# A pre-norm decoder layer on one core: loads split and reordered, buffer clearing moved, value projection written straight into two partition halves

## What is computed

```python
n = layernorm(x)
q, k, v = n @ Wq.T, n @ Wk.T, n @ Wv.T            # 16 heads of 16 features
s = q k^T / 4;  s = where(key > query, -inf, s) + alibi(head)
x = x + softmax(s) v @ Wo.T + bo
n = layernorm(x)
x = x + softmax(where(mask, n ctx^T / 16, -1e30)) ctx
n = layernorm(x)
up, down = mxfp4(W_up), mxfp4(W_down)             # block scales and 4-bit codes, blocks of 32 rows
x = x + gelu(n @ up) @ down + b_down
```

## Time and profile before

| | us |
|---|---|
| median of 3 runs | 162.13 |
| lowest and highest run | 159.33 and 162.51 |
| span of the profiled execution, first to last instruction | 157.1 |

### The profile page before, as it was taken

The page is one execution under the profiler, slowest core; times in us unless marked ns, Lnnn a source line. Parts: engine busy times, 40 slices in busy tenths (PEclk is TensorE's granted clock), DMA queues, the critical chain, the costliest instruction groups (busy, mean ns, idle before and its releaser), DMA issues. The chain is left out here.

```text
span 157.1 us, 2931 instructions
## 1 busy us (share of the span) xinstructions
PE 127.9 (81%) x878; PEld 87.3 (56%) x878; DVE 126.1 (80%) x345; ACT 96.4 (61%) x212; POOL 54.1 (34%) x92
## 2 busy tenths in 40 slices
PE   0149999987992497991977999898999999979992
PEld 0027444312471174550565657677788989759991
DVE  1854998799999999779899988796785789697551
ACT  3014559996936045582322742666989899899970
POOL 8969920052211240310403343732540254052000
PEclk9999999999999789998579999999999999999999
DMA  4999993000020341910000000000000000020011
GB/s 95 321 329 341 368 274 144 2 2 4 2 67 0 87 180 30 280 30 0 0 0 4 0 0 0 4 2 0 4 0 2 4 33 31 3 73 0 0 67 67
DMA packets 9135, 11.20 MB, mean 71 GB/s; under 512 B 1665, under 2 KB 7937, under 8 KB 8993
## 3 DMA queue, kind: packets, MB, share of 16 engines
q1 hardware_dynamic: 7776, 9.90, 20.3%
q10 hardware_dynamic: 1344, 1.13, 2.2%
HBM read 9.45 MB, written 1.05 MB: 67 GB/s over the span
## 5 line engine op out<-in xcount | busy, mean ns | idle before, releaser
L556 POOL TENSOR_TENSOR s_sb<-s_sb,s_max 128x512 f32<-128x512 f32 x16 | 17.3, 1084 | 50.1 <-DVE s_max L828 50.1
L969 PE MATMUL bank<-k,q_T 128*64 128x512 f32 x64 | 20.0, 681 | 5.2 <-DVE s_sb L825 5.2
L1064 PE MATMUL bank<-xn_T,w_T 128*128 128x256 f16 x128 | 19.2, 273 | 1.2 <-ACT h_sb L688 0.7
L1080 PE MATMUL bank<-w_down_q,h_hi 128*128 128x256 f32 x64 | 18.7, 318 | 0.0
L636 ACT ACTIVATE p_T<-bank 128x512 f32<-128x512 f32 x16 | 9.6, 599 | 13.1 <-PE bank L990 10.3
L932 PE MATMUL bank<-const,xn 128*128 128x128 f32 x48 | 10.3, 304 | 8.8 <-DVE xn L785 8.7
L990 PEld LDWEIGHTS bank<-v,p_T 128*64 128x64 f32 x256 | 14.1, 148 | 5.9 <-issue 4.7
L902 DVE TENSOR_TENSOR h_lo<-h_sb,h_hi 128x256 fp32r<-128x256 f32 x32 | 13.4, 437 | 4.8 <-ACT h_sb L688 4.8
L528 POOL TENSOR_SCALAR var_eps<-mean_var 128x1 f32<-128x1 f32 x24 | 5.8, 240 | 31.7 <-DVE mean_var L777 31.6
L688 ACT ACTIVATE h_hi<-bank,bias_cols 128x256 fp32r<-128x256 f32 x32 | 15.3, 478 | 2.3 <-PE bank L1080 0.7
L990 PE MATMUL bank<-v,p_T 128*64 128x34 f32 x256 | 15.7, 235 | 1.2 <-ACT q_T L643 1.1
(11 more groups left out here) (82 smaller groups left out, 271.6 us busy)
## 6 DMA issues: line engine op xcount, KB each, us to landing
raw<-in_W_up_T_dram SPq DMA_DIRECT2D x1, 1024.0 KB, 10.5
ctx_T<-in_ctx_by_feature_dram SPq DMA_DIRECT2D x1, 1024.0 KB, 9.7
ctx_sb<-in_ctx_dram SPq DMA_DIRECT2D x1, 1024.0 KB, 9.9
raw<-in_W_up_dram SPq DMA_DIRECT2D x1, 1024.0 KB, 4.9
raw<-in_W_down_T_dram SPq DMA_DIRECT2D x1, 1024.0 KB, 4.8
raw<-in_W_down_dram SPq DMA_DIRECT2D x1, 1024.0 KB, 6.6
out_dram<-x_sb SPq DMA_DIRECT2D x8, 128.0 KB, 1.7
x_sb<-in_x_dram SPq DMA_DIRECT2D x4, 128.0 KB, 3.1
```

The costliest lines, as they stand in the source:

```text
L556: pool.tensor_tensor(tile, tile, s_max[:, u % S_RING, :].unsqueeze(2).broadcast_to([P, HC, S]), ALU.subtract).then_inc(centred, 1)
L969: last = pe.matmul(dst[b * S:(b + 1) * S, :].rearrange("p (h k) -> p h k", h=HC), q_T[:, c, tok], k2[:, c, :, tok], start=True, stop=True)
L1064: last = pe.matmul(dst[:, 0:GN], w_up_q[:, c, f * P:(f + 1) * P], xn_T16[:, g * GT:(g + 1) * GT, at16:at16 + P], start=(k == 0), stop=(k = ...
L1080: last = pe.matmul(dst, src[:, i % H_RING, t * P:(t + 1) * P], w_down_q[:, f, :], start=(f == 0 and part == 0 and t == 0), stop=(f == FC - ...
```

## The change

It has four parts.

Loads: Wv is loaded alone, first behind the constants; then the bias columns, Wq and Wk, and Wo alone. SP waits for Wv before it issues x tiles 4 to 7 and all that follows, and alibi goes ahead of W_up_T. The semaphore for Wv and Wo becomes two.

Clearing: in the planner `x_fill` and the `v2_zero` of the second half come after the last `add_bo`. The instructions are the same.

Values: the rows of Wv are ordered on the host so that all even heads come first, then all odd ones. `v` uses 64 tokens of one sequence as weights and 128 columns of Wv as the moving operand, and writes even heads (j = 0) into partitions 0 to 63 of the bank and odd heads into 64 to 127: 16 calls for a pair of tiles in place of 4. One copy on ACT (`v_even`) and one on DVE (`v_odd`), each of 64 partitions by 512, then fill `v2`. `v_copy`, `v_own`, `v_move`, `v_spread` and the buffers `v_out` and `v_moved` are gone.

Order: some costs in `stages()` and nearly all weights in `URGENCY` are new.

```diff
@@ -85,11 +85,11 @@
             add("low", (t,), "dve", 0.35, [("turn_copy", (n, t))])
 
     for t in range(HALF + 1):
-        add("load_x", (t,), "dma", 2.3 if t == 0 else 0.9 if t < HALF else 2.5)
-
-    queues = {"dma": (("load_x", 0.0), ("load_row_biases", 0.6), ("load_rows", 0.6), ("load_up", 3.5),
-                      ("load_alibi", 1.0), ("load_mask", 1.0), ("load_ctx", 6.0)),
-              "dma2": (("load_biases", 4.0), ("load_qk", 3.0), ("load_vo", 1.5))}
+        add("load_x", (t,), "dma", 2.0 if t == 0 else 0.7 if t < HALF else 2.5)
+
+    queues = {"dma": (("load_x", 0.0), ("load_row_biases", 0.6), ("load_rows", 0.6), ("load_alibi", 1.0),
+                      ("load_up", 3.5), ("load_mask", 1.0), ("load_ctx", 6.0)),
+              "dma2": (("load_v", 4.5), ("load_biases", 0.2), ("load_qk", 1.5), ("load_o", 3.0))}
     for queue, loads in queues.items():
         before = []
         for name, us in loads:
...
@@ -118,13 +118,12 @@
                 add("k_rest", (h, c), "dve", 0.46 * (HC - K_HEADS[h, c]), [("k_flat", (h, c)), ("qk_bias", ())])
             keys[h, c] = copies
         for pair in range(2):
-            add("v", (h, pair), "pe", 1.75, turned[:2 * pair + 2] + [("load_vo", ())], [v_bank(h, pair)], ("v_own", (h, pair)))
-            add("v_copy", (h, pair), "act", 0.55, [("v", (h, pair))] + ([("v_move", (0,))] if h else []))
-            add("v_own", (h, pair), "dve", 0.7, [("v_copy", (h, pair)), ("v2_zero", (h,))])
-        add("v_move", (h,), "sp", 2.5, [("v_copy", (h, 1))] + ([("v_spread", (0,))] if h else []))
-        add("v_spread", (h,), "act", 1.0, [("v_move", (h,)), ("v2_zero", (h,))])
-        add("v2_zero", (h,), "pool", 2.6)
-    add("x_fill", (), "pool", 0.9)
+            add("v", (h, pair), "pe", 1.75, turned[:2 * pair + 2] + [("load_v", ())], [v_bank(h, pair)],
+                [("v_even", (h, pair)), ("v_odd", (h, pair))])
+            add("v_even", (h, pair), "act", 0.55, [("v", (h, pair)), ("v2_zero", (h,))])
+            add("v_odd", (h, pair), "dve", 0.6, [("v", (h, pair)), ("v2_zero", (h,))])
+        add("v2_zero", (h,), "pool", 2.6, [("add_bo", (TILES - 1,))] if h else [])
+    add("x_fill", (), "pool", 0.9, [("add_bo", (TILES - 1,))])
     add("rows_copy", (), "act", 1.1, [("load_rows", ())])
     add("qk_bias", (), "dve", 0.4, [("load_biases", ())])
 
...
@@ -140,13 +139,13 @@
         add("prob_copy", (u,), "act", 0.5, [("prob_T", (u,))] + ([("pv", (u - 2,))] if u >= 2 else []))
 
         reused = [("attn_turn", (u - 2,))] if u >= 2 else []
-        add("pv", (u,), "pe", 0.6, [("prob_copy", (u,)), ("v_spread", (h,)), ("v_own", (h, 1))] + reused, [4],
+        add("pv", (u,), "pe", 0.6, [("prob_copy", (u,)), ("v_even", (h, 1)), ("v_odd", (h, 1))] + reused, [4],
             ("normalise", (u,)))
         add("normalise", (u,), "dve", 0.45, [("pv", (u,))])
         add("attn_turn", (u,), "pe", 0.08, [("normalise", (u,))], [ATTN_BANK], ("attn_copy", (u,)))
         add("attn_copy", (u,), "act", 0.27, [("attn_turn", (u,))])
     for t in range(TILES):
-        add("out_proj", (t,), "pe", 0.9, [("attn_copy", (EC * t + EC - 1,))], [5], ("x1", (t,)))
+        add("out_proj", (t,), "pe", 0.9, [("attn_copy", (EC * t + EC - 1,)), ("load_o", ())], [5], ("x1", (t,)))
         add("x1", (t,), "dve", 0.4, [("out_proj", (t,)), ("add_bo", (t,))])
         layer_norm(LN2, t, [("x1", (t,))])
         add("x_scores", (t,), "pe", 0.45, [("turn_copy", (LN2, t)), ("load_ctx", ())], [7], ("x_mask", (t,)))
...
@@ -212,12 +211,16 @@
 PE_BUSY = 0.385
 
 URGENCY = {
-    "x_fill": 23, "add_down": 23, "v2_zero": 22, "norm": 18, "q": 17, "turn": 16, "attn_copy": 14,
-    "load_qk": 12, "final": 9, "load_mask": 6, "load_vo": 6, "spread_copy": 5, "pv": 5, "gelu": 5,
-    "out_proj": 3, "turn_copy": 3, "low": 3, "normalise": 2, "k_flat": 1, "prob_copy": 1, "x2": 1,
-    "load_rows": 0, "x_prob_copy": 0, "k_rest": 0, "x_read": -1, "stats": -1, "qk_bias": -1, "k_copy": -1,
-    "x_scale": -2, "q_copy": -2, "rstd": -2, "add_bo": -2, "x_mask": -2, "split": -2, "v_own": -4,
-    "scale_T": -9, "prob_T": -12,
+    "turn_copy": 78, "load_v": 52, "v_even": 48, "x_fill": 38, "x_read": 35, "attn_turn": 33, "normalise": 30,
+    "k_rest": 28, "load_o": 27, "split": 23, "amax": 23, "load_ctx": 22, "norm": 21, "centre": 19, "gelu": 18,
+    "prob_copy": 17, "x_mask": 17, "x1": 16, "x_prob_T": 15, "spread_copy": 13, "store": 13, "reload": 13,
+    "load_qk": 12, "low": 12, "rstd": 10, "add_down": 7, "turn": 7, "final": 6, "load_vo": 6, "load_rows": 3,
+    "spread": 3, "up": 3, "x_scores": 3, "q_copy": 2, "attn_copy": 1, "load_alibi": -1, "v2_zero": -2,
+    "x_exp": -3, "pv": -4, "add_bo": -4, "v_own": -4, "load_row_biases": -7, "load_up": -8, "load_biases": -10,
+    "quant": -13, "out_proj": -15, "load_mask": -16, "scores": -16, "down": -16, "x2": -19, "scale_T": -19,
+    "prob_T": -20, "k_copy": -26, "exp": -26, "k": -26, "load_x": -27, "binade": -29, "v_odd": -32,
+    "x_prob_copy": -39, "k_flat": -41, "qk_bias": -42, "q": -43, "add_max": -43, "scale_copy": -44,
+    "x_table": -59, "v": -100, "x_scale": -165,
 }
 
 
...
@@ -455,6 +451,15 @@
             return xn_T[:, h * HALF:(h + 1) * HALF, c * P:(c + 1) * P]
+
+        def v2_tiles(h, pair):
+
+            first = h * B // 2 + 4 * pair
+            return v2[:, first:first + 4, :, :, :]
+
+        def v_tiles(h, pair):
+
+            return bank[v_bank(h, pair)][:, :].rearrange("p (b g d) -> p b g d", b=4, d=D)
 
         def keys_copied(h, c):
...
@@ -466,14 +471,15 @@
         def _(sp):
             for t in range(HALF):
                 sp.dma_start(x_sb[:, t, :], x_tiles[t]).then_inc(x_loaded[t], 16)
+            sp.wait_ge(v_loaded, 16)
             sp.dma_start(x_sb[:, HALF:TILES, :], x_tiles[HALF:TILES].rearrange("t p e -> p t e")).then_inc(
                 x_loaded[HALF], 16)
             sp.dma_start(row_biases_all[:, :, :], row_biases.unsqueeze(0).broadcast_to([P, 2, E])).then_inc(
                 bias_loaded, 16)
             sp.dma_start(rows_f, block_of_row).then_inc(rows_loaded, 16)
+            sp.dma_start(alibi_sb[:, :, :], alibi).then_inc(alibi_loaded, 16)
             sp.dma_start(raw[:, :].rearrange("p (c k) -> p c k", c=FC),
                          W_up_T.rearrange("(c p) k -> p c k", p=P)).then_inc(raw_loaded, 16)
-            sp.dma_start(alibi_sb[:, :, :], alibi).then_inc(alibi_loaded, 16)
             for b in range(2):
                 sp.dma_start(mask_u8[b * S:(b + 1) * S, :, :],
                              ctx_mask.rearrange("(t b) s -> b t s", b=2)[b].unsqueeze(0).broadcast_to([S, TILES, S])
@@ -481,16 +487,6 @@
             sp.dma_start(ctx_T[:, :, :, :], ctx_by_feature).then_inc(ctx_loaded, 16)
             sp.dma_start(ctx_sb[:, :, :], ctx.rearrange("(t b) s e -> (b s) t e", b=2)).then_inc(ctx_loaded, 16)
             for stage, at in order:
-                if stage == "v_move":
-
-                    h = at[0]
-                    sp.wait_ge(v_copied, 2 * (h + 1))
-                    if h == 1:
-
-                        sp.wait_ge(v2_moved, 2)
-                    for b in range(2):
-                        sp.dma_start(v_moved[(1 - b) * S:(2 - b) * S, :, :],
-                                     v_out[b * S:(b + 1) * S, :, :]).then_inc(v_loaded[h], 16)
                 if stage == "reload":
 
...
@@ -559,9 +555,10 @@
         @block.scalar
         def _(act):
             act.dma_start(const[:, :], ident_heads).then_inc(const_loaded, 16)
+            act.dma_start(w_T[:, WV, :, :], W_vo_T[0].rearrange("(i p) o -> p i o", p=P)).then_inc(v_loaded, 16)
             act.dma_start(bias_cols[:, :], biases).then_inc(bias_cols_loaded, 16)
             act.dma_start(w_T[:, WQ:WK + 1, :, :], W_qk_T.rearrange("m (i p) o -> p m i o", p=P)).then_inc(qk_loaded, 16)
-            act.dma_start(w_T[:, WV:WO + 1, :, :], W_vo_T.rearrange("m (i p) o -> p m i o", p=P)).then_inc(vo_loaded, 16)
+            act.dma_start(w_T[:, WO, :, :], W_vo_T[1].rearrange("(i p) o -> p i o", p=P)).then_inc(o_loaded, 16)
 
             for stage, at in order:
                 if stage == "turn_copy":
@@ -599,30 +596,15 @@
                                               ACT.Identity, bias=bk_masked[:, c, head:head + 1],
                                               scale=head_mask[:, head:head + 1])
                     last.then_inc(k2_ready[c], 1)
-                if stage == "v_copy":
+                if stage == "v_even":
                     h, pair = at
+                    act.wait_ge(v2_zeroed, h + 1)
                     act.wait_ge(v_ready, 2 * h + pair + 1)
-                    if h == 1 and pair == 0:
-
-                        act.wait_ge(v_loaded[0], 32)
-                    for b in range(2):
-                        last = act.activation(
-                            v_out[b * S:(b + 1) * S, 2 * pair:2 * pair + 2, :].rearrange("p t (g d) -> p t g d", d=D),
```

(47 more changed lines are left out.)

11 lines of the change are left out of this document (3 added, 8 removed).

## The result

The changed kernel takes 164.19 us (median of 4 runs, 163.46 to 164.67), the kernel before 160.73 in runs beside it: ratio 1.034, 95% interval 1.026 to 1.042. The changed kernel is slower, and the forecast of 156.4 and its range are missed. The profiled execution took 163.46 us for a span of 161.7, so 1.8 us lie outside the span. The spans themselves were 157.1 and 161.7: 4.6 us more, where 151.4 was forecast.

A forecast was written before the change was run, and what follows sets the result against it. No engine was full: a late start, then VectorE from 30 to 90 us, then TensorE set the pace. −3.8 + 0.2 − 0.6 + 0.5 − 2.0 = −5.7 us gave span 151.4, plus 5.0: 156.4 us; range 151.0 to 161.0.

The forecast's parts named there:

- A value stage at full clock: Value projection on TensorE: 32 records of 128 columns forecast at 2.0 us, against 1.89 before; 3.8 without overlap.
- rival C: Value projection: the two partition halves run one after another, each stage +1.9 us, total 162.9; chance 0.07.
- VectorE's value copies: VectorE loses 8 × 0.417 us of copies and gets 4 at 0.68: −0.6 us, on the bound.
- 3.8 us earlier, and with it the transposes of tiles 2 and 3 and q(0,0), near 12.7: Start: v(0,0) at 7.3 instead of 11.11 through loading V alone, following TensorE work moving with it: −3.8 us.
- the price of the fills beside the key copies: Mask-table fill and second clear on GpSimd, moved near VectorE's key copies: cost 0 to 2.87 us, taken as 0.5.
- B: Rival: start won but given back, order brings nothing and fills block key copies for 2.87 us: 160.8; chance 0.18.
- The order: −2.0 forecast: New stage order over the whole span: between 6.3 us gained and 6.9 lost, taken as −2.0.
- The hole at 74: TensorE's 2.90 us wait until 73.92 for a normalise behind the third quantisation; the new weights were expected to work against it.
- 5.16 + 1.7: Price of one new hole like TensorE's wait until 53.15, idle time plus low-clock loss: 6.9 us worse.
- 2.90 + 3.4: Worth of removing TensorE's wait until 73.92, idle time plus low-clock loss: up to 6.3 us.
- 5.0 us that I put outside the span: Median of the runs, 162.13, less the profiled span, 157.1; added to the forecast span of 151.4.
- D: Rival, slower: two quantisations together ahead of an add_max make holes of 6.9 us each; 165.3 or 172.2; chance 0.08.

The follow-up runs named there:

- h: Changed kernel with the mask-table fill behind the first clear, second clear behind rstd of tile 3, `rows_copy` behind the copy of tile 3: 161.4 us, 1.012.
- d: Kernel before with only the new order of stages, its loads, value path and early clearing kept: 165.2 us, ratio 1.030.
- v: Changed kernel with 16, 12 and 12 added identity turns on TensorE ahead of three long-waiting turns of attention results: 163.46 us, ratio 1.033.
- w: e with identity turns added on TensorE, 20 ahead of scores(7) and 11 ahead of attn_turn(2): 159.95 us, ratio 1.008.
- e: Kernel before with only the new value path; loads, order and clearing as they were: 159.3 us, ratio 0.998.
- a: Changed kernel with only the fill and second clear put back where the kernel before has them: 162.6 us, ratio 1.013.
- b: Changed kernel in the order of the kernel before, fill and second clear still behind the last `add_bo`: 162.5 us, ratio 1.014.
- c: Changed kernel with both the order and the place of fill and clear undone, new loads and values kept: 159.7 us, ratio 0.996.
- s1: e without the arithmetic of W_down's two quantisations but for their last multiplication: 152.88 us, ratio 0.951.
- s2: h without the arithmetic of W_down's two quantisations but for their last multiplication: 154.88 us, ratio 0.962.
- o: e with W_down's two quantisations moved on VectorE behind normalise(7) and normalise(8), as in the changed kernel: 167.92 us, ratio 1.047.
- m: h with W_down's two quantisations moved ahead, behind add_max(10) and add_max(11): 167.63 us, ratio 1.047.
- g: Changed kernel's loads and values, h's start up to the first k projection, then the order of the kernel before: 160.05 us, ratio 0.998.
- k: g with the W_up maxima moved behind the first key copies on VectorE: 160.38 us, ratio 1.000.

## Why the prediction was wrong

**What stood.** The start to the first value stage: norm 0 ended at 5.35 (5.24 forecast), v(0,0) began at 7.54 (7.3) and took 3.68 (4.0). x 4 to 7 came in time, statistics at 10.32 (11.5). A value stage at full clock took 1.92 to 1.97 us (2.0), so the halves run side by side and rival C is out:

```profile
34.26 1.95 PE L933 MATMUL bank<-w_T,xn_T 128*64 128x128 f32 x32
```

VectorE's value copies ahead of the cut went from 3.3 us to 2.8: −0.5 (−0.6). These are right terms of a wrong sum.

**The start, carried on to the first add_max.** By the sum it would have been at 31.06 − 3.8 + 0.2 + 0.5 = 28.0; it was at 32.55. Two steps failed.

The first is "3.8 us earlier, and with it the transposes of tiles 2 and 3 and q(0,0), near 12.7". It carried the whole gain past two loads whose landing did not move: x tiles 4 to 7 (10.4 and 10.3) and the block rows (12.0 and 12.2). I judged them by when their data is needed, not by what stands behind `rows_copy` on ScalarE and behind the transposes of tile 4 on TensorE. The first projection began at 14.39, 1.7 late, and it was k(0,0): the new order puts both k stages of this half ahead of q(0,0), which ran only at 20.03. h, without `rows_copy` in the way, has 14.18; how the 1.7 us divide between the two waits is not shown.

The second is the price of the fills beside the key copies, with bounds of 0 and 2.87 us, "I take 0.5": the copies were stretched by 3.95, beyond the upper end. The bound counted the instructions that move, and put the fills ahead of the copies ("the fills come some 2 us before VectorE's key copies"). But the copies came 4.9 us earlier (18.20 against 23.05), and `add_bo`, which the fills wait for, ended only 0.4 us earlier (20.60 against 21.00). So the copies met the last additions, and then both fills from start to end. h shows that `add_bo` alone makes 1.6 of it. The Trainium skill (SBUF — State Buffer, "Who interferes with whom") says that a VectorE operation of the tensor_scalar kind, in a two-port mode, and a GpSimd one block each other whole, whichever begins second. The trace agrees in direction: GpSimd is busy 5.91 us beside the copies, and they are stretched by 3.95. B's mechanism was real, and larger than B had it.

**The order: −2.0 forecast.** Alone it costs 3.0% (d). I read it from weights, for one hole. The hole at 74 went, but the wait for a normalise behind a quantisation came back in three other places. The price I gave such a hole was wrong too, "5.16 + 1.7" and "2.90 + 3.4", idle time plus half clock. v and w show that the half clock costs little while VectorE is full; that the idle time of TensorE costs nothing there either is read from VectorE's 13.62 busy of 14.00 us, not tried. The new order also delays the start, by 1.4 us in d. What must be priced is VectorE's time ahead of up(0). From the first add_max to up(0) it took 73.7 us before and 76.6 after; VectorE's busy time in it:

```profile
31.10:104.80 73.70, 59.49 (x419) 35.70 (x417) 67.71 (x177) 38.16 (x81) 23.08 (x30) 0.93 0.13 37
```

and in the changed kernel:

```profile
32.50:109.10 76.60, 61.80 (x505) 39.02 (x506) 69.37 (x178) 32.73 (x72) 22.97 (x28) 0.87 0.13 42
```

VectorE is busy 1.7 us more and idle 1.2 more. The trace suggests where the 1.7 come from. A multiplication of 128x1 elements, 0.16 us long, takes 1.03 where GpSimd's subtraction began 0.02 us ahead of it; the last of these pairs ahead of the cut, in the changed kernel:

```profile
98.81 1.04 POOL L552 TENSOR_TENSOR s_sb<-s_sb,s_max 128x512 f32<-128x512 f32 x1 [13.25 <-DVE s_max L804]
98.83 1.03 DVE L852 TENSOR_TENSOR xs_scale<-xs_inv,valid 128x1 f32<-128x1 f32 x1
```

It happens three times ahead of up(0), at 74.90, 98.83 and 104.08, and once before, at 88.38. Two more at 0.87 us are 1.7. The weight of `x_scale`, −165, puts it right behind the row maximum of an add_max, which is what releases the subtraction. This is read, not tried: no run moved `x_scale` alone. d has the same three and nearly the same sum (69.63 us busy in 77.5). But other groups differ too, by up to 0.9 us either way (the maxima for the quantisations 2.5 to 3.4 us, the first step of the quantisations 4.7 to 3.9). And h, with the same three pairs against e's one, is busier than e by 0.9 us only (69.30 against 68.39). So the pairs are a part of the cost, of a size that is not shown.

**The account.** The span was forecast at 151.4 and came to 161.7, 10.3 more: 4.5 up to the first add_max (28.0 against 32.55), 5.5 from there to up(0) (73.7 − 0.6 − 2.0 = 71.1 against 76.6), 0.3 behind it. In the time, part of this was hidden by the 5.0 us that I put outside the span: the changed kernel and every other profiled execution have 1.8 to 2.2 there. 162.13 was the middle of three runs of a kernel that scatters from 157.9 to 165.3 beside the experiments; a profiled execution of span 157.1 stands for some 159.

**The rivals.** D named the right side but asked for a hole of 6.9 us; the holes are there (3.79, 2.90, 2.80), but VectorE is nearly full around the last two (13.62 of 14.00 us from 90 to 104). The change is slower because B's loss was larger than all that was left of the start's gain (a, b, c, h) and because the new order costs 3% by itself (d); how the order does it is known only in part.

**What stays open.** Of the order's cost, 1.2 us of VectorE's idle time in the changed kernel (1.9 in d) have no single cause, and the busy time was not traced by a run: s1 and s2 say that it isn't W_down's quantisation, v that the clock is a small part at most. Why o and m lost 6 to 9 us is open too. No version beat the kernel before: e, c, g and k lie between 0.996 and 1.000 of it, and only c's interval ends below 1, at 0.9997.

## What to carry to other kernels

When one engine is full up to some point and the time behind that point is fixed, price a change by that engine's busy and idle time up to it, and only then by the waits of the others. Before work of GpSimd is moved, or VectorE's work is made earlier, list all that GpSimd runs in the new place, not only what moves. When a start is moved earlier, look for loads that will not land earlier, and at what their consumers block on their own engines: the gain ends at the first of them.

## What the runs showed of the hardware

A VectorE multiplication of 128x1 with two inputs in SBUF took 1.03 us instead of 0.16 where a GpSimd subtraction of 1.04 us had begun 0.02 to 0.03 us before it, and 0.73 beside an addition of 0.72 at 134.54. The Trainium skill (SBUF — State Buffer, "Who interferes with whom") says that a VectorE instruction with two SBUF inputs contends with a GpSimd one that reads SBUF; the trace agrees in these cases. It doesn't in this one of the changed kernel, where the GpSimd operation on 128x1 had begun 0.10 us before and the multiplication was not held up:

```profile
132.72 0.57 POOL L528 TENSOR_TENSOR rstd<-var_eps,minus_half 128x1 f32<-128x1 f32 x1
```

```profile
132.82 0.16 DVE L852 TENSOR_TENSOR xs_scale<-xs_inv,valid 128x1 f32<-128x1 f32 x1
```

Five tensor_scalar copies of 128x512 float32 took 2.37 us alone, 4.01 beside five additions on GpSimd, and 6.32 beside additions and two memsets.

With work in TensorE's waits the granted clock behind them rose from 0.68 to 1.00 in w and from 0.50 and 0.52 to 0.76 in v. It brought no time in w and 0.7 us at most in v, where VectorE was nearly full.

SP issued the block rows 1.9 us later than before, and they landed 0.2 us later (12.2 against 12.0).

A stage of 32 records with 64 weight columns and 128 moving ones, alternating between the halves of a bank, takes 1.92 to 1.97 us at full clock and 3.68, about half that pace, in the start; the 8 records of 256 columns that it replaces took 1.89 and 3.78. The slow pace of the start is not in the granted clock that the profile gives, 1.00 from 7.5 to 11.3 us after and from 11 to 15 before; its cause is open.
